# A perceiver layer on one core: time mixing taken into the attention loop, and a context copy moved from VectorE to ScalarE

## The chip, the cores and the metric

One NeuronCore of a Trainium2 chip. The time is that of one execution on the device in microseconds (us); the value for a kernel is the median of its runs. PE is TensorE, DVE is VectorE, ACT is ScalarE, POOL is GpSimd, SP is the engine that issues most DMAs.

## What is computed

The input x has 128 sequences of 32 tokens of width 128, the context 128 times 257 rows of width 96. Three residual blocks follow one another:

```python
x = x + xattn(layernorm(x), ctx)      # 16 heads, softmax over the 257 context rows
x = x + time_mix(layernorm(x))        # along the 32 tokens of a sequence
x = x + moe(layernorm(x))             # 8 experts, one is chosen for each token

# time_mix, x_prev is x shifted by one token:
k, v, r = ((x*mix + x_prev*(1-mix)) @ W.T for each of key, value, receptance)
ek = exp(k);  f_a = ek*v / a_next;  f_b = headsum(ek) / a_next
state = nan_to_num(a_pow * exclusive_cumsum(f))        # for a and b, along the tokens
out = sigmoid(r) * (state_a + eu*ek*v) / max(state_b + eu*headsum(ek), 1e-6) @ W_out.T
```

## The kernel before, in words

All 4096 tokens stay in SBUF as 32 tiles of 128 (`X`); a tile holds the 32 queries of four sequences. The five engines each have a program of their own, written out by hand; they meet at semaphores, and each engine runs its instructions strictly in the order in which they are written.

**Attention** is a loop over the 128 sequences (`pipeline`, L576; eight steps `j` = -1 to 6 in one iteration `it`, sequence n = 8*it + j). In step n PE (`pe_step`, L423) transposes the context of sequence n+2 (L360), multiplies the scores of n+1 in four tiles (L371), where the fourth tile reuses bank 0 of the first and so waits until its exponential has been taken (L369), projects the queries of n+5 into bank 3 (L383), multiplies probabilities and context of n-1 (L394, L400), in one step of four (the ones with j = 1 and 5, "projection steps") projects the output of a tile with 48 matmuls (L408), and transposes the leftovers (L449) and the probabilities of n in two halves (L416). DVE (`dve_step`, L494) copies the transposed context out of bank 7 (`dve_cT`, L533), takes the maxima (L511) and the low halves (L507, L491, L530), adds the residual of a tile (L526) and takes the statistics for the next layer norm (L623) in the step behind. ACT (`act_step`, L456) copies the high halves of the transposed probabilities (L462), takes the four exponentials (L468), and copies the queries' (L486) and the output's high halves (L477). POOL (`pool_step`, L553) normalises the probabilities (L559) and splits the context in high and low halves (L541, L545).

**Time mixing** comes after the last attention residual: tables and transposed weights (L1028 to L1039, L901 to L914, L1170 to L1183), then a pipeline over eight chunks of 512 tokens with `pe_mix` (L1041), `act_mix` (L916), `dve_mix` (L1185) and `pool_mix` (L808) in five banks of their own. Its arrays share their place in SBUF with those of the attention. Its weights are loaded early (L700 to L706), on SP's queue behind the first contexts. The expert weights are loaded once the last attention residual is done (L712 to L723).

**Routing and experts** follow: layer norm, router, sorting through DRAM, and a loop over 40 tiles of tokens with expert weights chosen at run time.

## Time and profile before

| | us |
|---|---|
| median of three runs | 1127.61 (1126.6 to 1131.02) |
| the profiled execution's own time | 1121.37 |
| its span, first to last instruction | 1119.7 |
| busy: PE, DVE, ACT, POOL | 921.9, 856.5, 665.6, 634.8 |

The page of the profile gives busy times, the chain that ended last and the costliest groups. A stretch is a window of the span, with each engine's busy time in it and the clock that PE was granted (1.00 is 2.4 GHz; 0.50 is 1.2 GHz; values between are mixtures). A timeline lists instructions with start and duration; successive ones on an engine overlap a little, so that the distance between two starts, and not the duration, is what one more of them costs. An idle time is put down to what released the engine. POOL's spans are rough.

### The profile page before, as it was taken

How to read it: one execution, taken by the hardware profiler on the slowest of the kernel's cores; microseconds unless marked ns; L12 is line 12 of the kernel's file. 1: busy time of each engine (PE TensorE's matmuls, PEld its weight loads, DVE VectorE, ACT ScalarE, POOL GpSimd, SP SyncE). 2: the span in 40 equal slices, each digit the busy share in tenths (PEclk: the TensorE clock that was granted, in tenths of full speed). 3: DMA queues.
4: the chain of work that ended last, by engine and by line, in shares of the span. 5: the costliest groups of instructions: out<-in, count | busy, mean ns of one | idle time of the engine just before them, and what ended most of it. 6: DMA issues, size and time to landing. Idle time of an engine off the chain costs nothing.

```text
span 1119.7 us, 30693 instructions
## 1 busy us (share of the span) xinstructions
PE 921.9 (82%) x9018; PEld 759.3 (68%) x9019; DVE 856.5 (76%) x2288; ACT 665.6 (59%) x1892; POOL 634.8 (57%) x983
## 2 busy tenths in 40 slices
PE   3899999999999999999999999965444436148885
PEld 3788888888888888888888888742222236136664
DVE  5888878878888887888888788757999976225543
ACT  2677767777776776777777677643121202136664
POOL 4466666665666666566566666626575510735453
PEclk9899999999999999999999999987676655659888
DMA  6100010010000001001000100039000000111110
GB/s 176 25 16 17 16 28 14 14 29 14 14 20 23 14 15 29 14 14 28 15 14 15 29 14 15 3 72 195 0 1 0 0 0 3 53 46 48 42 44 17
DMA packets 46488, 32.13 MB, mean 29 GB/s; under 512 B 6518, under 2 KB 44065, under 8 KB 46448
## 3 DMA queue, kind: packets, MB, share of 16 engines
q1 hardware_dynamic: 44144, 27.38, 10.0%
q0 software_dynamic: 2304, 4.25, 1.1%
q8 instruction: 20, 0.33, 0.1%
q14 instruction: 20, 0.16, 0.0%
HBM read 24.62 MB, written 7.52 MB: 29 GB/s over the span
## 4 chain that ended last, share of the span: by engine, by line
PE 72%; DVE 13%; issue 9%; ACT 3%; DMA 1%; POOL 1%; SPq 1%; ACTq 0%; DVEq 0%; POOLq 0%
PE bank L371 15%; PE bank L394 15%; PE bank L416 10%; PE bank L408 8%; PE bank L383 7%; DVE cs L1234 4%; PE bank L1114 4%; PE bank L1129 3%; PE bank L400 3%; PE bank L360 2%; DVE xn L656 1%; PE bank L663 1%; PE bank L1084 1%; DVE den L1225 1%; DMA wo_r<-in_L_xattn_Wo_dram 1%
## 5 line engine op out<-in xcount | busy, mean ns | idle before, releaser
L559 POOL TENSOR_TENSOR Pn<-Pe,rsum 128x1028 f32<-128x1028 f32 x128 | 243.1, 1899 | 226.6 <-DVE rsum L518 142.3
L468 ACT ACTIVATE Pe<-bank,nmax 128x257 f32<-128x257 f32 x512 | 239.5, 471 | 92.5 <-DVE nmax L511 92.4
L511 DVE TENSOR_REDUCE nmax<-bank 128x1 f32<-128x257 f32 x512 | 199.2, 409 | 1.2 <-PE bank L371 1.2
L371 PE MATMUL bank<-cT,qh 96*128 96x257 f16 x1024 | 185.2, 275 | 5.1 <-ACT Pe L468 4.1
L462 ACT ACTIVATE Th<-bank 128x512 f16<-128x512 f32 x256 | 138.9, 595 | 78.9 <-PE bank L416 78.9
L507 DVE TENSOR_TENSOR Tl<-bank,Th 128x512 f16<-128x512 f32 x256 | 172.8, 676 | 0.0
L371 PE MATMUL bank<-cT,ql 96*128 96x257 f16 x512 | 139.1, 272 | 0.0
L416 PE MATMUL bank<-identf,Pn 128*128 128x128 f32 x1024 | 133.5, 273 | 0.0
L416 PEld LDWEIGHTS bank<-identf,Pn 128*128 128x128 f32 x1024 | 109.8, 141 | 0.0
L491 DVE TENSOR_TENSOR ql<-bank,qh 96x512 f16<-96x512 f32 x128 | 87.9, 687 | 23.5 <-ACT qh L486 23.5
L468 ACT ACTIVATION_READ_ACCUMULATOR Pe<-bank,nmax 128x1 f32 x512 | 99.9, 195 | 0.0
L530 DVE TENSOR_TENSOR Ol<-bank,Oh 96x512 f16<-96x512 f32 x128 | 87.6, 685 | 12.4 <-ACT Oh L477 4.5
L371 PEld LDWEIGHTS bank<-cT,qh 96*128 96x128 f16 x1024 | 83.7, 97 | 18.8 <-issue 5.4
L383 PE MATMUL bank<-x1h,Ahi 128*96 (+1 forms) x512 | 93.5, 221 | 0.0
L383 PE MATMUL bank<-x1h,Alo 128*96 (+1 forms) x512 | 93.3, 220 | 0.0
L383 PE MATMUL bank<-x1l,Ahi 128*96 (+1 forms) x512 | 93.2, 220 | 0.0
L408 PE MATMUL bank<-Bhi,Oh 96*128 96x128 f16 x512 | 87.5, 219 | 1.5 <-DVE Ol L530 1.5
L408 PE MATMUL bank<-Bhi,Ol 96*128 96x128 f16 x512 | 87.4, 219 | 0.0
L408 PE MATMUL bank<-Blo,Oh 96*128 96x128 f16 x512 | 87.3, 219 | 0.0
L522 DVE COPY L<-bank 128x128 f16<-128x128 f16 x128 | 25.5, 200 | 73.1 <-PE bank L449 73.1
L477 ACT ACTIVATE Oh<-bank 96x512 f16<-96x512 f32 x128 | 75.8, 592 | 4.2 <-PE bank L400 3.2
L394 PE MATMUL bank<-Th,chi 128*96 128x512 f16 x256 | 76.6, 379 | 0.9 <-DVE Ol L530 0.9
(221 smaller groups left out, 2478.1 us busy)
## 6 DMA issues: line engine op xcount, KB each, us to landing
raw<-in_ctx_dram SPq DMA_DIRECT2D x32, 384.0 KB, 3.3
sorted_rows<-fill SPq DMA_DIRECT2D x1, 2620.0 KB, 20.8
xs<-sorted_rows SPq DMA_DIRECT2D x40, 65.5 KB, 1.8
R<-in_x_dram SPq DMA_DIRECT2D x4, 512.0 KB, 5.9
Z<-last_rows SPq DMA_DIRECT2D x128, 2.2 KB
w1r<-in_L_ffn_W_dram SPq DMA_DIRECT2D x8, 256.0 KB, 6.0
w2fr<-in_L_ffn_W_dram SPq DMA_DIRECT2D x8, 256.0 KB, 6.3
out_dram<-yout,idx POOLq DMA_INDIRECT x40, 2.3
```

The source lines that it names most:

```text
L371: last = nc.tensor.matmul(bank[SB[t]][:, 0:M], w[:, par, b, t * P:(t + 1) * P], cT[:, s4, c, 0:M], start=(k == 0), stop=(k == 2))
L383: last = nc.tensor.matmul(bank[b][0:CC, hh * P:(hh + 1) * P], w[:, h, :], a[:, tok], start=(k == 0), stop=(k == 2))
L394: nc.tensor.matmul(bank[6][0:CC, :], w[:, s8, c, :], p[:, par, c, :], start=(k == 0), stop=False)
L408: last = nc.tensor.matmul(bank[7][:, 512 - C:512], o[:, gp, h, :], w[:, h, :], start=(h == 0 and k == 0), stop=(h == H - 1 and k == 2))
L416: last = nc.tensor.transpose(bank[4 + c][:, t * P:(t + 1) * P], Pn[:, par, t, c * P:(c + 1) * P], identf[:, :])
L462: nc.scalar.activation(Th[:, n_par(j - 1), c, :], bank[4 + c][:, :], ACT.Copy).then_inc(s_Th, 1)
L468: nc.scalar.activation(Pe[:, n_par(j + 1), t, :], bank[SB[t]][:, 0:M], ACT.Exp, bias=nmax[:, n_par(j + 1), t:t + 1], accum_out=sums[:, n_p ...
L491: nc.vector.tensor_tensor(q_view(ql, par, c), bank[b][0:CC, :].rearrange("p (h b t) -> p h b t", h=QT, b=GB), q_view(qh, par, c), ALU.subt ...
L507: nc.vector.tensor_tensor(Tl[:, n_par(j - 1), t, :], bank[4 + t][:, :], Th[:, n_par(j - 1), t, :], ALU.subtract).then_inc(s_Tl, 1)
L511: nc.vector.tensor_reduce(nmax[:, n_par(j + 1), t:t + 1], bank[SB[t]][:, 0:M], AX.X, ALU.max, negate=True).then_inc(s_nmax, 1)
L530: nc.vector.tensor_tensor(Ol[sl], bank[6][0:CC, :].rearrange("p (h t) -> p h t", h=H), Oh[sl], ALU.subtract).then_inc(s_Ol, 1)
L559: nc.gpsimd.tensor_tensor(Pn[:, par, :, :], Pe[:, par, :, :], rsum[:, par, :].unsqueeze(2).broadcast_to([P, QT, M]), ALU.mult)\
```

## The change

Time mixing is cut into 16 chunks of 256 tokens (two tiles, eight sequences), and each chunk's operations are placed at the ends of the steps of the attention loop, one iteration for one chunk and spread over three iterations. Chunk c has its normalisation at j=3 of iteration c+1, transposes at 4, k at 5, its sum at 6, v and r at j=-1 and 0 of iteration c+2, the scans at 1 and 2, and so on to the output at j=1 of iteration c+3. PE's part lies between the two halves of the probabilities' transposes, in bank 3, which the queries' projection uses as well; that one now waits until the chunk's result has been read. The other engines' parts stand at the end of their steps. The normalisation moves from DVE to POOL, with a power and one Newton step in place of ACT's square root; DVE adds an aggregation (`bn_aggr`). The context copy moves from DVE to ACT, behind the copies of the probabilities. Tables and transposed weights are made before the loop. After the loop a remainder (`drain_mix`) runs what is left of the last chunks. The same buffers serve every chunk (the key, value and sum arrays were doubled before), and the code of the first three iterations is written out instead of one. The functions called anew are all in the diff; `...` marks lines left out.

```diff
             if exists(n + 5):
-
+                pe_mix_free(it, j)
                 pe_q(n + 5, (j + 1) % GB, bass.ds(P * (g + 1 + (jj + 1) // GB), P))
...
                 wait(nc.tensor, s_pn, n + 1)
-                pe_probsT(n, n_par(j))
+                pe_probsT(n, n_par(j), 0)
+            pe_mix(it, j, n)
+            if exists(n):
+                pe_probsT(n, n_par(j), 1)
+
+        def chunk(it, back):
+            c = it - back
+            return c if exists(c, MCH) else None
+
+        def pe_mix_free(it, j):
+
+            if j == 5 and chunk(it, 1) is not None:
+                wait(nc.tensor, s_m["xc"], it)
...
+        def pe_mix_bank(it, j, n):
+
+            if exists(n + 5):
+                wait(nc.tensor, s_ql, n + 6)
+            else:
+                wait(nc.tensor, s_ql, B)
+                pe_mix_free(it, j)
+
+        def pe_mix(it, j, n):
+            if j == 4 and chunk(it, 1) is not None:
+                c = it - 1
+                pe_mix_bank(it, j, n)
+                wait(nc.tensor, s_m["xn"], c + 1)
+                for t in range(MG):
+                    last = nc.tensor.transpose(bank[3][:, t * P:(t + 1) * P], xn2[:, t, :], identf[:, :])
+                last.then_inc(s_m["xT"], 1)
+            if j == 5 and chunk(it, 1) is not None:
+                c = it - 1
+                pe_mix_bank(it, j, n)
+                wait(nc.tensor, s_m["xc"], c + 1)
+                nc.tensor.matmul(bank[3][:, 0:MT], wka[:, :], xT33[:, :, 1:N + 1], start=True, stop=False)
+                nc.tensor.matmul(bank[3][:, 0:MT], wkb[:, :], xT33[:, :, 0:N], start=False, stop=True)\
+                    .then_inc(s_m["k"], 1)
...
+                nc.tensor.matmul(bank[3][:, 0:MT], blk[:, :], ek[:, :], start=True, stop=True).then_inc(s_m["sum"], 1)
...
+                nc.tensor.matmul(bank[3][:, 0:MT], w2T[:, 1, :], xm[:, 0, :], start=True, stop=True).then_inc(s_m["v"], 1)
...
+                nc.tensor.matmul(bank[3][:, 0:MT], w2T[:, 2, :], xm[:, 1, :], start=True, stop=True).then_inc(s_m["r"], 1)
...
+                for t in range(MG):
+                    last = nc.tensor.matmul(bank[3][:, t * P:(t + 1) * P], oT[:, t * P:(t + 1) * P], w2T[:, 3, :],
+                                            start=True, stop=True)
+                last.then_inc(s_m["y"], 1)
...
                     nc.scalar.activation(Th[:, n_par(j - 1), c, :], bank[4 + c][:, :], ACT.Copy).then_inc(s_Th, 1)
+            if exists(n + 2):
+                act_cT(n + 2, (j + 2) % 4)
...
+            act_mix(it, j)
+
+        def act_cT(n, s4):
+            wait(nc.scalar, s_ctxT, n + 1)
+            nc.scalar.activation(cT[:, s4, :, 0:MC * P], bankh[7][0:CC, 0:2 * MC * P].rearrange("p (s m) -> p s m", s=2),
+                                 ACT.Copy).then_inc(s_cT, 1)
...
+        def act_mix(it, j):
...
+                wait(nc.scalar, s_m["xT"], c + 1)
+                nc.scalar.activation(xT33[:, :, 1:N + 1], time(bank[3][:, 0:MT]), ACT.Copy).then_inc(s_m["xc"], 1)
...
+                wait(nc.scalar, s_m["ekv"], c)
+                wait(nc.scalar, s_m["k"], c + 1)
+                nc.scalar.activation(ek[:, :], bank[3][:, 0:MT], ACT.Exp).then_inc(s_m["ek"], 1)
+                wait(nc.scalar, s_m["xm"], 2 * c)
+                wait(nc.scalar, s_m["dx"], c + 1)
+                for k in range(2):
+                    last = nc.scalar.activation(mdx[:, k, :], dx[:, :], ACT.Copy, scale=mix[:, 1 + k:2 + k])
...
+                wait(nc.scalar, s_m["sum"], c + 1)
+                nc.scalar.activation(esum[:, :], bank[3][:, 0:MT], ACT.Copy).then_inc(s_m["esum"], 1)
...
+                wait(nc.scalar, s_m["r"], c + 1)
+                nc.scalar.activation(er[:, :], bank[3][:, 0:MT], ACT.Exp, scale=-1.0).then_inc(s_m["er"], 1)
+                wait(nc.scalar, s_m["dm"], c)
+                wait(nc.scalar, s_m["er"], c + 1)
+                nc.scalar.activation(er1[:, :], er[:, :], ACT.Copy, bias=1.0).then_inc(s_m["er1"], 1)
...
             moments = jj == 2 and exists(g - 1, G)
             if moments:
                 wait(nc.vector, s_res, g)
-            if exists(n + 2):
-                dve_cT(n + 2, (j + 2) % 4)
-            if moments:
-                dve_stats(g - 1)
-
+                wait(nc.vector, s_m["mv"], g - 2)
+                wait(nc.vector, s_m["xd"], it - (1 if j == 2 else 0))
...
+                if kind == "max" and t == 0 and moments:
+                    nc.vector.bn_stats(stats2[:, 1 - gp, :],
+                                       X[:, bass.ds(g - 1, 1), :].rearrange("p o c -> p (o c)")).then_inc(s_m["stat"], 1)
...
+            if moments:
+                wait(nc.vector, s_m["stat"], g)
...
+            if moments:
+                nc.vector.bn_aggr(mv[:, 1 - gp, :], stats2[:, 1 - gp, :]).then_inc(s_m["mv"], 1)
+            dve_mix(it, j)
+
+        def dve_mix(it, j):
+            if j == 2 and chunk(it, 3) is not None:
...
+                for t in range(MG):
+                    nc.vector.bn_stats(stats[:, bass.ds(MG * c + t, 1), :].rearrange("p o s -> p (o s)"),
+                                       X[:, bass.ds(MG * c + t, 1), :].rearrange("p o c -> p (o c)")).then_inc(s_m["stat3"], 1)
+            if j == -1 and chunk(it, 2) is not None:
...
+                wait(nc.vector, s_m["v"], c + 1)
+                nc.vector.tensor_tensor(ekv[:, :], ek[:, :], bank[3][:, 0:MT], ALU.mult).then_inc(s_m["ekv"], 1)
+            if j in (1, 2) and chunk(it, 2) is not None:
+                c, k = it - 2, j - 1
+                wait(nc.vector, s_m["st"], 2 * c)
+                wait(nc.vector, s_m["fab"], 2 * c + k + 1)
+                for b in range(MS):
+                    last = nc.vector.tensor_tensor_scan(cs[:, k, b, 1:N + 1], onesn[:, :], fab[:, k, b * N:(b + 1) * N],
+                                                        0.0, ALU.mult, ALU.add)
...
+                wait(nc.vector, s_m["y"], c + 1)
+                xc = X[:, bass.ds(MG * c, MG), :]
+                nc.vector.tensor_tensor(xc, xc, bank[3][:, 0:MT].rearrange("p (t c) -> p t c", t=MG), ALU.add)\
+                    .then_inc(s_m["res"], 1)
+            if j == 3 and chunk(it, 2) is not None:
...
+                    nc.vector.tensor_scalar(scl[:, k, :], sraw[:, k, :], -FMAX, FMAX, ALU.max, ALU.min)\
+                        .then_inc(s_m["scl"], 1)
...
+                    nc.vector.scalar_tensor_tensor(sst[:, k, :], sraw[:, k, :], FMAX, scl[:, k, :],
+                                                   ALU.is_le, ALU.mult).then_inc(s_m["sst"], 1)
+            if j == 4 and chunk(it, 2) is not None:
...
+                nc.vector.scalar_tensor_tensor(den[:, :], esum[:, :], nlw[:, 1:2], sst[:, 1, :], ALU.mult, ALU.add)\
...
+                nc.vector.scalar_tensor_tensor(num[:, :], ekv[:, :], nlw[:, 1:2], sst[:, 0, :], ALU.mult, ALU.add)\
...
+                nc.vector.scalar_tensor_tensor(denm[:, :], den[:, :], 1e-6, er1[:, :], ALU.max, ALU.mult)\
+                    .then_inc(s_m["dm"], 1)
+            if j == 5 and chunk(it, 2) is not None:
...
+                wait(nc.vector, s_m["dm"], c + 1)
+                nc.vector.reciprocal(rec[:, :], denm[:, :]).then_inc(s_m["rec"], 1)
...
+        def pool_mix(it, j):
+            if j == 3 and chunk(it, 1) is not None:
+                c = it - 1
+                wait(nc.gpsimd, s_m["mv"], MG * (c + 1))
...
+                nc.gpsimd.tensor_tensor(vep[:, :], mv[:, :, 1], consts[:, 0, :], ALU.add).then_inc(s_m["rs"], 1)
+                nc.gpsimd.tensor_tensor(xd[:, :, :], X[:, bass.ds(MG * c, MG), :],
+                                        mv[:, :, 0:1].broadcast_to([P, MG, C]), ALU.subtract).then_inc(s_m["xd"], 1)
+                wait(nc.gpsimd, s_m["rs"], r + 1)
+                nc.gpsimd.tensor_tensor(rs0[:, :], vep[:, :], consts[:, 1, :], ALU.pow).then_inc(s_m["rs"], 1)
+                nc.gpsimd.tensor_tensor(rsv[:, :], vep[:, :], consts[:, 1, :], ALU.mult).then_inc(s_m["rs"], 1)
+                wait(nc.gpsimd, s_m["rs"], r + 3)
+                nc.gpsimd.tensor_tensor(rsq[:, :], rs0[:, :], rs0[:, :], ALU.mult).then_inc(s_m["rs"], 1)
+                wait(nc.gpsimd, s_m["rs"], r + 4)
+                nc.gpsimd.tensor_tensor(rsv[:, :], rsq[:, :], rsv[:, :], ALU.mult).then_inc(s_m["rs"], 1)
+                wait(nc.gpsimd, s_m["rs"], r + 5)
+                nc.gpsimd.tensor_tensor(rsc[:, :], rsv[:, :], consts[:, 2, :], ALU.add).then_inc(s_m["rs"], 1)
+                wait(nc.gpsimd, s_m["rs"], r + 6)
+                nc.gpsimd.tensor_tensor(rst2[:, :], rs0[:, :], rsc[:, :], ALU.mult).then_inc(s_m["rs2"], 1)
+                wait(nc.gpsimd, s_m["rs2"], c + 1)
+                wait(nc.gpsimd, s_m["xd"], c + 1)
+                nc.gpsimd.tensor_tensor(xn2[:, :, :], xd[:, :, :], rst2[:, :].unsqueeze(2).broadcast_to([P, MG, C]),
+                                        ALU.mult).then_inc(s_m["xn"], 1)
+            if j == 5 and chunk(it, 1) is not None:
...
+                nc.gpsimd.tensor_tensor(time(dx[:, :]), xT33[:, :, 1:N + 1], xT33[:, :, 0:N], ALU.subtract)\
+                    .then_inc(s_m["dx"], 1)
+            if j == 6 and chunk(it, 1) is not None:
...
+                for k in range(2):
+                    nc.gpsimd.tensor_tensor(time(xm[:, k, :]), time(mdx[:, k, :]), xT33[:, :, 0:N], ALU.add)\
...
+                wait(nc.gpsimd, s_m["ekv"], c + 1)
+                nc.gpsimd.tensor_tensor(time(fab[:, 0, :]), time(ekv[:, :]), over_seqs(iap[:, 1:N + 1]), ALU.mult)\
+                    .then_inc(s_m["fab"], 1)
+                wait(nc.gpsimd, s_m["esum"], c + 1)
+                nc.gpsimd.tensor_tensor(time(fab[:, 1, :]), time(esum[:, :]), over_seqs(iap[:, 1:N + 1]), ALU.mult)\
+                    .then_inc(s_m["fab"], 1)
+            if j in (1, 2) and chunk(it, 2) is not None:
...
+                nc.gpsimd.tensor_tensor(time(sraw[:, k, :]), cs[:, k, :, 0:N], over_seqs(apw[:, 0:N]), ALU.mult)\
+                    .then_inc(s_m["st"], 1)
+            if j == 6 and chunk(it, 2) is not None:
...
+                nc.gpsimd.tensor_tensor(oT[:, :], num[:, :], rec[:, :], ALU.mult).then_inc(s_m["o"], 1)
...
-            for j in range(-1, 7):
-                step(0, j)
-            with eng.Fori(1, B // 8 - 1) as it:
+            for i in range(3):
+                for j in range(-1, 7):
+                    step(i, j)
+            with eng.Fori(3, LIT - 1) as it:
                 for j in range(-1, 7):
                     step(it, j)
-            for j in range(-1, 10):
-                step(B // 8 - 1, j)
+            for j in range(-1, 7):
+                step(LIT - 1, j)
+            for j in range(-1, 2):
+                step(LIT, j)
+
+        def drain_mix(step):
+            for j in range(2, 7):
+                step(LIT, j)
+            for j in range(-1, 7):
+                step(LIT + 1, j)
+            for j in range(-1, 3):
+                step(LIT + 2, j)
...
+            drain_mix(pool_step)
...
+            act.wait_ge(s_w2T, 1)
+            nc.scalar.activation(w2T[:, :, :].rearrange("p a c -> p (a c)"), bank[3][:, :], ACT.Copy).then_inc(s_w2Tc, 1)
+            act.wait_ge(s_w2, 16 * (7 + 2 * HS))
+            nc.scalar.activation(nlw[:, :], dcy[:, :], ACT.Exp).then_inc(s_texp, 1)
+            act.wait_ge(s_tdve, 2)
+            act.wait_ge(s_tab, 1)
+
+            nc.scalar.activation(apw[:, :], tt[:, :], ACT.Exp, scale=nlw2[:, 0:1])\
+                .then_inc(s_texp, 1)
+            act.wait_ge(s_m["zero"], 2)
             pipeline(nc.scalar, act_step)
...
+            drain_mix(act_step)
+
+
+            act_std(2)
...
-            pipeline(nc.tensor, pe_step)
...
             pe.wait_ge(s_w2, 16 * (7 + 2 * HS))
             for a in range(4):
-                last = nc.tensor.transpose(bank[1][:, a * P:(a + 1) * P], w2r[:, a, :], identf[:, :])
+                last = nc.tensor.transpose(bank[3][:, a * P:(a + 1) * P], w2r[:, a, :], identf[:, :])
             last.then_inc(s_w2T, 1)
+            pe.wait_ge(s_w2Tc, 1)
+            pe.wait_ge(s_tab, 5)
+            pe.wait_ge(s_m["w"], 2)
+            pipeline(nc.tensor, pe_step)
+            pe.wait_ge(s_res, G)
...
+            drain_mix(pe_step)
...
+            dve_tables()
             pipeline(nc.vector, dve_step)
-
-
-            dve.wait_ge(s_res, G)
-            dve_stats(G - 1)
-            dve_var(chain, LS)
+            drain_mix(dve_step)
+
+
+            dve.wait_ge(s_m["stat3"], G)
+            dve_var(chain, LS - G)
             dve_rstd(chain, 2)
```

## Rows read from the trace of the kernel before

**Rows 1.** Stretches: us, then each engine's busy us (instructions), clock, DMA share, GB/s.

```profile
100.00:400.00 300.00, 299.50 (x3253) 258.04 (x3252) 254.82 (x641) 227.16 (x671) 190.21 (x333) 1.00 0.06 18
...
800.00:900.00 100.00, 44.33 (x108) 24.32 (x108) 99.83 (x286) 19.17 (x32) 58.66 (x41) 0.66 0.00 0
...
1040.00:1050.00 10.00, 8.48 (x87) 6.88 (x86) 5.07 (x18) 6.34 (x21) 4.28 (x6) 0.83 0.16 48
```

**Rows 2.** Timeline where the attention ends: start, us, instruction, idle before and releaser.

```profile
744.03 0.29 DVE L526 TENSOR_TENSOR R<-R,bank 128x128 f32<-128x128 f32 x1 [3.02 <-PE bank L408]
```

**Rows 3.** The chain that ended last, in the time-mixing stage: start, us, what.

```profile
773.36 1.72 PE bank L1051 x2
...
911.10 0.88 DVE stats L623 x4
```

**Rows 4.** Timeline of PE, one step of the attention loop.

```profile
413.03 0.28 PE L360 MATMUL bank<-ident,chi 128*96 128x128 f16 x2
...
414.93 0.40 PE L371 MATMUL bank<-cT,qh 96*128 96x257 f16 x2
...
416.84 1.04 PE L416 MATMUL bank<-identf,Pn 128*128 128x128 f32 x8
417.73 0.28 PE L360 MATMUL bank<-ident,chi 128*96 128x128 f16 x2
```

**Rows 5.** Timeline of DVE, a projection step's end and the same plain step.

```profile
402.74 0.23 DVE L522 COPY L<-bank 128x128 f16<-128x128 f16 x1 [2.31 <-PE bank L449]
...
413.53 0.41 DVE L535 COPY cT<-bank 96x512 f16<-96x512 f16 x1
413.86 0.74 DVE L511 TENSOR_REDUCE nmax<-bank 128x1 f32<-128x257 f32 x2
...
417.62 0.69 DVE L530 TENSOR_TENSOR Ol<-bank,Oh 96x512 f16<-96x512 f32 x1
```

**Rows 6.** Timeline of ACT, the same step.

```profile
414.31 0.48 ACT L468 ACTIVATE Pe<-bank,nmax 128x257 f32<-128x257 f32 x1 [0.42 <-DVE nmax L511]
414.68 0.19 ACT L468 ACTIVATION_READ_ACCUMULATOR Pe<-bank,nmax 128x1 f32 x1
...
415.56 0.47 ACT L468 ACTIVATE Pe<-bank,nmax 128x257 f32<-128x257 f32 x1 [0.24 <-DVE nmax L511]
...
416.99 0.59 ACT L477 ACTIVATE Oh<-bank 96x512 f16<-96x512 f32 x1
417.49 1.09 ACT L462 ACTIVATE Th<-bank 128x512 f16<-128x512 f32 x2
```

**Rows 7.** Timeline of POOL, the work that the same step ends with.

```profile
417.49 1.90 POOL L559 TENSOR_TENSOR Pn<-Pe,rsum 128x1028 f32<-128x1028 f32 x1 [1.04 <-DVE rsum L518]
419.47 0.21 POOL L566 TENSOR_TENSOR e12p<-Pn,one 128x8 f16<-128x8 f32 x1
419.76 0.20 POOL L569 TENSOR_TENSOR e12p<-Pn,e12p 128x4 f16<-128x4 f32 x1
...
420.99 0.19 POOL L551 COPY cT<-c256T 96x2 f16 x1
```

**Rows 8.** Groups of instructions by form, 770 to 925 us: busy us, mean ns.

```profile
L1234 DVE TENSOR_TENSOR_SCAN cs<-onesn,fab 128x32 f32<-128x32 f32 x227 | 40.0, 255 | 0.0
L1228 DVE RECIPROCAL rec<-den 128x512 f32<-128x512 f32 x8 | 26.8, 3353 | 0.3
...
L835 POOL TENSOR_TENSOR xm<-mdx,xT 128x512 f32<-128x512 f32 x12 | 16.5, 1393 | 0.0
...
L1209 DVE SCALAR_TENSOR_TENSOR sst<-sraw,scl 128x512 f32<-128x512 f32 x16 | 10.3, 680 | 0.0
...
L937 ACT ACTIVATE mdx<-dx,mix 128x512 f32<-128x512 f32 x12 | 7.9, 711 | 0.0
```

**Rows 9.** One line's instructions (the denominator's product): ns min/median/max, first and last start.

```profile
L1225 DVE SCALAR_TENSOR_TENSOR den<-den,er x8: 683/1584/1584, 778.0 to 902.7; 128x512 f32<-128x512 f32 x8
```

**Rows 10.** Timeline of the SP queue, the last loads before the loop.

```profile
35.68 5.01 SPq L706 DMA_DIRECT2D dcy<-n_L_attn_time_first_dram  x8
```

370 lines of the change are left out of this document (154 added, 216 removed).

## The prediction, made before the change was run

> **What bounds the kernel now.** I read the page first, then stretches, the hand-over between the stages, and last one step of the attention loop on each engine. Inside the loop PE is busy for 299.50 of 300 us at full clock (2.4 GHz); from 800 to 900 us it is DVE that never rests (99.83 of 100 us), while PE works less than half of the time at a granted clock of 0.66, parts at 2.4 and parts at 1.2 GHz [rows 1]. So there are two stages with two bounds. The time-mixing stage lies between the residual of the last attention tile at 744.03 [rows 2] and the end of the last statistics at 911.10 + 0.88 [rows 3]: **168.0 us**, with nothing of the attention beside it. That is all the change can take away.
>
> One step of the loop, counted from its first context transpose (413.03 = 0; the next step begins at 417.73): period **4.70**, the last score tile at 1.90, the transposes of the probabilities from 3.81 to 4.70 [rows 4]. A step with the output projection has 48 matmuls more, start to start 0.056, so 2.7 us. Eight steps are 43.3 us. Three things matter for any work added here.
> - The last score tile reuses the bank of the first and waits for its exponential, which starts at 1.28 and whose accumulator read ends at 1.84 [rows 6]; PE comes free of the queries' projection at 1.89. **There is no slack:** whatever makes the first exponential late by x stops PE for x.
> - DVE: the context copy begins at 0.50, the first maximum at 0.83, the last subtraction at 4.59; marginal cost of the copy 0.33 [rows 5]. Without it DVE could start the maximum at 0.53 (0.49 and the hand-over). The exponential follows its start by 0.45, so it must start by about 0.82: DVE has 0.3 us to give per step. In a projection step DVE idles 2.31 us before its copy of the leftovers, but work placed at the end of a step comes behind that wait.
> - ACT: idle 0.42 before the first exponential and 0.24 before the third [rows 6]. Its 96x512 copy costs 0.50 (416.99 to 417.49).
>
> POOL's work of a step runs from 417.49 to 421.18, that is 3.69 of 4.70 us, and lies across the step boundary (from -0.24 to 3.46) [rows 7].
>
> **The context copy on ACT.** 0.50 fits into 0.66 idle; behind the two probability copies it ends at about 1.26, where the first exponential started anyway. Nothing gained or lost in a plain step, and ACT has no slack left. It removes a small delay in the step behind a projection, where DVE had statistics in front of the first maximum: -0.3 per eight steps.
>
> **PE's share of a chunk.** A 512-column f32 matmul is two instructions that took 1.72 us at half clock [rows 3], so 256 columns take 0.43 at full. Five of them (2.13), two transposes (the eight of a step take 4.70 - 3.81 = 0.89: 0.22), and two 128-column output matmuls (0.43): **2.8 us** per eight steps.
>
> **Stalls in a full iteration**, prices halved from [rows 8], each as the lateness of the next first exponential.
> - j=-1, ekv on DVE: 0.35, less than DVE's slack and PE's longer step: 0.
> - j=0: ACT waits for r, then er and, dependent, er1. Probability copies start at 0.52 instead of -0.24: **0.75** (0.4 to 0.8).
> - j=1: eight scans at 0.18 and a residual of 0.35 on DVE; maximum at 1.75, 0.93 too late. Beside POOL the scans take 0.24: 1.4. I take **1.2**.
> - j=2: aggregation, two statistics and eight scans, 2.1: 1.8, beside POOL 2.25. I take **2.0**.
> - j=3: two clamps and two selections, 1.05 to 1.55: **1.0** (0.5 to 1.3).
> - j=4: POOL's normalisation is nine operations, seven of them tiny and mostly dependent; POOL starts a dependent tiny one 0.29 after another (419.47 to 419.76) [rows 7]. With two 256-column operations of 0.6 to 0.7 (half of 1393 ns [rows 8]): 3.2 us from 3.46, ready at 6.7, while PE wants it at about 5.3. The power has no row; between 0.2 (a tiny one) and 0.8. Wait **1.2** (0.3 to 2). den, num and denm (1.2 to 2.4) hide mostly in it; **0.3** is left, also for ACT's copy.
> - j=5: on ACT ek behind k, then two mdx of some 0.37 (half of 711 ns [rows 8]) that wait for POOL's dx, which ends some 0.65 into the next step: **1.6** (0.9 to 1.9). The reciprocal on DVE, half of 3353 ns [rows 8], is 0.45 late and hidden by this; without that cover it costs 0.45.
> - j=6: esum on ACT behind the sum: **0.3**.
>
> These are 8.35; low ends 4.7, high ends 10.5. With PE's 2.8 and the -0.3 a full iteration grows by **10.85 us**, and 13 of the 16 are full: 141. Partial ones, by the same terms: the first with a chunk (only j=3 to 6) 4.9, the next (no output matmuls, residual or statistics) 9.7, the three last steps 3.0. Together **158.6**.
>
> POOL beside DVE: denm takes 683 ns alone and mostly 1584 ns beside POOL [rows 9]; that is the upper end above. The Trainium skill ("GPSIMD Engine Reference", Key points) says that the engine shares its SBUF interfaces with VectorE and collides with VectorE instructions with two SBUF inputs; by that rule scans, selections and the three denominators would all be slow beside the normalisation of the probabilities, and the sum would stand near its high ends. The trace agrees for denm.
>
> **Before and behind the loop.** Weights and tables must now be ready first. The last decay load is issued at 40.69 [rows 10], lands some 2 us later, when the loop begins (43.3), so loads cost little; but transposes (0.7), copy (0.6), table load (1.28), exponentials, reciprocal and two scalings (some 2) then stand in a row in front of PE: **4.5** (3 to 6; the table load was hidden before). Behind the loop the last chunk runs alone: POOL's tables and normalisation 7, transposes and copy 1.3, k at half clock 1.7, ek and sum 1.6, xm and v 1.9, ekv and fab 1.8, two rounds of scans and scalings 4.4, clamps to denominators 2.4, reciprocal 1.8, oT 0.7, output and residual 1.4, statistics 0.5: **26.5** (22 to 34). The expert weights' loads begin after the attention as before and have 60 us instead of 200; they needed about 35 us, so nothing.
>
> **Sum:** 158.6 + 4.5 + 26.5 - 168.0 = **+21.6 us**. The profiled execution took 1121.4 (span 1119.7), so 1143; it lies 6.2 below the median of 1127.6, to which I add: **1149**. Low ends: 105 + 3 + 22 - 168 = -38, 1090. High ends: 195 + 6 + 34 - 168 = +67, 1195.
>
> **Rivals.**
> 1. *The engines soak the chunk up; faster.* The place is the wait of the last score tile. If stalls are at their low ends (256-column operations cheaper than halved rows, POOL's chain in time), the iteration grows by 7.2: **1090**. It decides where an iteration grows by less than (168.0 - 26.5 - 4.5 - 17.6) / 13 = 9.2 us; my sum is 1.65 above that. For it: DVE's whole demand would be about 43 of 54 us, ACT's less; so a little run-ahead pays. Against: DVE and ACT work in order, and the added work stands just in front of the tightest hand-over. If only PE's 2.8 counted it would be 1035, which I hold for unlikely.
> 2. *The clock.* PE would be busy 46 of 54 us, 85%. In a stretch of the expert stage at 85% (8.48 of 10 us) it had 0.83 of full clock [rows 1], so parts at 1.2 GHz. PE's 46 us at that clock, less what the stalls cover, are 3.5 more per iteration: **1195**. Against: dense bursts of 4 us between the gaps. [...]
> 3. *ACT becomes the bound everywhere,* as the moved copy doesn't fit: 0.1 to 0.2 in 128 steps, **1168**. For: 0.02 us of slack. Against: the sum of the row starts just fits.
>
> **Chances.** Forecast 0.37, rival 1 0.38 (its middle at 1090, spread over both sides of it), rival 2 0.15, rival 3 0.10. About 0.5% (5.6 us) is what a measurement of this kernel can tell from no change. Faster by more than that: 0.34 of rival 1 and 0.02 of the forecast, 0.36. Within: 0.04 and 0.05, 0.09. Slower: 0.30 + 0.15 + 0.10, 0.55. The signs are both likely; the forecast's own range is 1125 to 1175. The range for 8 in 10 is 1078 to 1195: the low side holds rival 1 with half of its error, the high side the forecast's high ends and rival 2.
>
> **What would show it.** Right: the loop's steps at j=2, 3, 5 of an iteration longer by 1 to 2 us, with PE waiting for ACT's first exponential; that one waiting for DVE's maximum after j=1 to 3, and for ACT's own queue after j=0 and 5; PE waiting for POOL's normalised chunk at j=4; an iteration of 54 us; PE 85% busy in the loop; some 27 us between the last attention residual and the last statistics; the loop beginning 4.5 us later. Wrong: an iteration under 52 us (rival 1), a granted clock under 0.95 in the loop (rival 2), or plain steps longer than 4.75 (rival 3).

## The result, and the profile after

The changed kernel takes **1167.97 us** (median of four runs, 1163.18 to 1169.5); the kernel before, on the same chip, 1127.11 (1121.29 to 1131.02). The ratio is 1.036 with a 95% interval of 1.0304 to 1.0415: slower, by 40.9 us. The forecast was 1149, the range 1078 to 1195.

The profiled execution took 1169.27 us, its span is 1167.5 (before: 1121.37 and 1119.7). Where the spans' 47.8 us are:

| stretch | before | after | difference | forecast |
|---|---|---|---|---|
| start to first step of the loop | 43.6 | 52.8 | +9.2 | +4.5 |
| loop, to the last attention residual | 700.4 | 875.9 | +175.5 | +158.6 |
| time mixing behind the loop | 168.0 | 30.3 | -137.7 | -141.5 |
| rest | 207.7 | 208.5 | +0.8 | 0 |

About 5 of the first row's 9.2 us are not the change's: the same setup matmuls took longer in this execution, at the lower level of the clock (last section). The second row holds 3 us of the clock too. PE stood still ahead of the first step, and that step then began at the lower level:

```profile
52.84 0.42 PE L377 MATMUL bank<-ident,chi 128*96 128x128 f16 x2 [3.90 <-issue]
```

```profile
52.30:62.50 10.20, 8.88 (x58) 7.33 (x59) 4.08 (x11) 6.17 (x18) 3.45 (x6) 0.50 0.01 2
```

Iteration 0 has no chunk in it and still took 42.66 us, where it took 39.65 before.

Stretches of the loop, columns as in [rows 1]; the first row answers to the first there:

```profile
100.00:400.00 300.00, 262.27 (x2708) 219.44 (x2706) 238.08 (x612) 215.22 (x616) 199.05 (x356) 1.00 0.06 16
400.00:700.00 300.00, 260.32 (x2637) 215.66 (x2636) 240.63 (x608) 210.01 (x600) 195.92 (x353) 0.99 0.05 15
```

PE, busy 299.50 of 300 us before, now has some 38 us of gaps in 300; no other engine is full, DVE is even less busy than before (254.82). The granted clock is 1.00 and 0.99 in these stretches, nearly all of the time the upper level. What opens the gaps, from the waits of 400 to 700 us (engine, line, what it waited for: us, times, longest):

```profile
PE bank L388 <- ACT Pe L555: 34.2, 33, 1.8
ACT Pe L555 <- DVE nmax L633: 30.1, 48, 2.1
PE bank L505 <- POOL xn L791: 5.2, 6, 1.1
ACT er L600 <- PE bank L528: 2.8, 5, 0.6
```

PE waits for ACT's first exponential, and ACT for DVE's first maximum. One step (j=3 into j=4) on four engines. PE, where in [rows 4] the last score tile came 1.90 after the step's start, then DVE, ACT and POOL, which answer to [rows 5 to 7]:

```profile
839.35 0.28 PE L377 MATMUL bank<-ident,chi 128*96 128x128 f16 x2
...
843.03 0.40 PE L388 MATMUL bank<-cT,qh 96*128 96x257 f16 x2 [1.63 <-ACT Pe L555]
...
846.62 0.41 PE L505 MATMUL bank<-identf,xn 128*128 128x128 f32 x2 [1.06 <-POOL xn L791]
```

```profile
839.24 0.69 DVE L657 TENSOR_TENSOR Ol<-bank,Oh 96x512 f16<-96x512 f32 x1
839.84 1.52 DVE L696 TENSOR_SCALAR scl<-sraw 128x256 f32<-128x256 f32 x2
841.29 0.76 DVE L701 SCALAR_TENSOR_TENSOR sst<-sraw,scl 128x256 f32<-128x256 f32 x2
841.97 0.74 DVE L633 TENSOR_REDUCE nmax<-bank 128x1 f32<-128x257 f32 x2
...
846.33 0.47 DVE L708 SCALAR_TENSOR_TENSOR den<-esum,nlw,sst 128x256 f32<-128x256 f32 x1
846.72 2.12 DVE L711 SCALAR_TENSOR_TENSOR num<-ekv,nlw,sst 128x256 f32<-128x256 f32 x1
848.77 0.42 DVE L716 SCALAR_TENSOR_TENSOR denm<-den,er 128x256 f32<-128x256 f32 x1
```

```profile
842.41 0.48 ACT L555 ACTIVATE Pe<-bank,nmax 128x257 f32<-128x257 f32 x1 [1.74 <-DVE nmax L633]
```

```profile
839.12 1.90 POOL L750 TENSOR_TENSOR Pn<-Pe,rsum 128x1028 f32<-128x1028 f32 x1 [2.24 <-DVE rsum L643]
...
843.83 0.70 POOL L779 TENSOR_TENSOR rs<-vep,consts 128x2 f32<-128x2 f32 x1
...
845.86 0.61 POOL L791 TENSOR_TENSOR xn<-xd,rst 128x256 f32<-128x256 f32 x1
846.43 2.13 POOL L750 TENSOR_TENSOR Pn<-Pe,rsum 128x1028 f32<-128x1028 f32 x1
```

Here the last score tile comes 3.68 after the step's start, 1.78 late. DVE had scl and sst between its last subtraction and the first maximum. The first two scl take 1.52 us and end at 841.36, 0.34 behind the end of POOL's Pn (839.12 + 1.90 = 841.02). num takes 2.12 us and ends 0.28 behind the next Pn (848.84 and 848.56). The same num over the whole run: shortest, median and longest in ns:

```profile
L711 DVE SCALAR_TENSOR_TENSOR num<-ekv,nlw,sst x16: 471/2120/2121, 182.7 to 953.2; 128x256 f32<-128x256 f32 x16
```

Ten of the 16 are held, 1.65 us beyond num's own 0.47. Of the other six, one belongs to the first chunk and two to the drain; in the other three den, just ahead of num, was the one held (1.17 and twice 1.7 us for 0.47). The subtraction Ol, which reads PSUM, runs beside Pn in its usual 0.69.

### The profile page after: what moved, and what is told of

It is laid out like the page before. It is cut to its first block, busy times and chain, and to the rows that moved or that the text cites. A ratio compares the mean times of both kernels' runs of the same rounds, so it can differ in the third digit from the quotient of the medians.

```text
span 1167.5 us, 31247 instructions
## 1 busy us (share of the span) xinstructions
PE 935.8 (80%) x9098; PEld 772.6 (66%) x9099; DVE 832.9 (71%) x2229; ACT 731.2 (63%) x2072; POOL 687.1 (59%) x1194
## 4 chain that ended last, share of the span: by engine, by line
PE 33%; POOL 25%; issue 20%; ACT 9%; DVE 8%; POOLq 1%; DMA 1%; ACTq 1%; SPq 1%; DVEq 0%
POOL Pn L750 11%; PE bank L411 7%; PE bank L388 4%; PE bank L425 4%; PE bank L1269 3%; POOL chi L732 3%; ACT Pe L555 2%; PE bank L432 2%; PE bank L1284 2%; POOL sorted_rows L1073 2%; ACT Th L547 2%; POOL e12p L757 1%; DVE nmax L633 1%; PE bank L917 1%; PE bank L400 1%
## 5 line engine op out<-in xcount | busy, mean ns | idle before, releaser
L750 POOL TENSOR_TENSOR Pn<-Pe,rsum 128x1028 f32<-128x1028 f32 x128 | 246.5, 1926 | 258.5 <-DVE rsum L643 220.3
L633 DVE TENSOR_REDUCE nmax<-bank 128x1 f32<-128x257 f32 x512 | 203.3, 412 | 42.5 <-PE bank L388 41.1
L432 PE MATMUL bank<-identf,Pn 128*128 128x128 f32 x1024 | 147.8, 273 | 0.0
L432 PEld LDWEIGHTS bank<-identf,Pn 128*128 128x128 f32 x1024 | 115.0, 142 | 5.9
L555 ACT ACTIVATION_READ_ACCUMULATOR Pe<-bank,nmax 128x1 f32 x512 | 102.8, 201 | 0.0
```

What stands on the lines that cost most here:

```text
L432: last = nc.tensor.transpose(bank[4 + c][:, t * P:(t + 1) * P], Pn[:, par, t, c * P:(c + 1) * P], identf[:, :])
L555: nc.scalar.activation(Pe[:, n_par(j + 1), t, :], bank[SB[t]][:, 0:M], ACT.Exp, bias=nmax[:, n_par(j + 1), t:t + 1], accum_out=sums[:, n_p ...
L633: nc.vector.tensor_reduce(nmax[:, n_par(j + 1), t:t + 1], bank[SB[t]][:, 0:M], AX.X, ALU.max, negate=True).then_inc(s_nmax, 1)
L750: nc.gpsimd.tensor_tensor(Pn[:, par, :, :], Pe[:, par, :, :], rsum[:, par, :].unsqueeze(2).broadcast_to([P, QT, M]), ALU.mult)\
```

## The experiments

The experiments ran in three groups, each on a chip of its own beside the kernel before. That kernel's medians there were 1128.04 (copy_alone, copy_back, scans_early, clamps_mid), 1130.04 (scans_mid, norm_split, act_late, spread) and 1127.8 us (dve_only, spread2, spread3, spread3_back). The changed kernel itself was measured only once, with the result above. The ratios have 95% intervals of about half a per cent to either side, so that 5 us between two experiments is the least that the medians alone can show, and across groups some us more. Where two medians are close I give beside them the *long stretch*, from the loop's first step to the end of the last statistics, read from the profiled executions: 906.2 us in the changed kernel and 868.3 in the one before. It leaves out the setup, which differs from one execution to the next (last section). Step lengths are medians over eleven iterations of the distances between PE's first context transposes:

```text
                 5     6    -1     0     1     2     3     4    iteration (mean of 13)
changed       9.23  6.65  5.65  5.34  8.54  5.19  6.80  7.95    55.20
copy_back     9.89  6.18  5.36  5.35  8.07  5.54  7.14  7.96    55.48
scans_early   9.22  6.64  5.65  5.34  9.87  4.81  4.90  7.95    54.11
scans_mid     9.22  6.65  5.65  5.34  8.54  4.78  4.90  7.96    52.80
clamps_mid    9.09  7.17  5.65  5.34  8.54  5.19  6.80  7.87    55.94
norm_split    9.64  6.65  5.65  5.34  8.54  5.19  6.80  6.86    54.57
act_late      9.22  5.78  5.36  5.34  7.98  5.19  6.80  7.95    53.56
dve_only      9.49 10.89  5.65  5.34  8.55  4.78  5.26  8.55    57.64
spread        8.41  5.46  5.37  5.34  7.98  4.78  5.26  6.77    49.56
spread2       8.27  5.47  5.36  5.34  7.99  4.78  5.26  5.94    48.37
spread3       8.27  5.47  5.36  5.35  7.98  4.78  5.25  5.94    48.35
spread3_back  8.27  5.55  5.37  5.34  7.82  4.87  5.58  5.93    48.69
```

My theory was that the stalls are a matter of order: work in front of DVE's first maximum or ACT's first exponential, lengthened by POOL's Pn. The rivals: the copy on ACT is what costs, or the amount of work is, in whatever order.

### The copy alone (copy_alone, copy_back)

```diff
 # copy_alone: the kernel before, act_step, behind the two copies Th
+            if exists(n + 2):
+                wait(nc.scalar, s_ctxT, n + 3)
+                nc.scalar.activation(cT[:, (j + 2) % 4, :, 0:MC * P], ..., ACT.Copy).then_inc(s_cT, 1)
 # and dve_step
-                dve_cT(n + 2, (j + 2) % 4)
```

> The kernel before, with the copy of the transposed context moved from DVE to ACT behind its copies of the probabilities, and nothing else. Theory (the copy fits into gaps that ACT has in a plain step, and the end-of-step work of the time mixing is what costs): the step stays at 4.70 us, the time within 6 us of 1127. Rival (ACT bounds the step once it has the copy): each of some 130 steps grows by 0.1 to 0.3 us, 1140 to 1165.

Measured: **1121.07**, ratio 0.9958 (0.9935 to 0.998). copy_back is the reverse edit on the changed kernel (`act_cT` out, `dve_cT` in at the start of DVE's step).

> The changed kernel with the copy of the context back on DVE, at the start of DVE's step. Theory (DVE's work between its last and its next maximum is what makes the last score tile late): about 0.6 us more of DVE in front of the first maximum of each step that follows mixing work, 0.3 to 0.6 us in 7 of 8 steps, 13 iterations: 27 to 55 us slower than the changed kernel, 1195 to 1222. Rival (the copy on ACT is what the change costs): faster than the changed kernel, 1125 to 1150.

Measured: **1173.51**, 5.5 us slower than the changed kernel. The long stretch is 862.9 us in copy_alone and 911.9 in copy_back, 5.5 shorter and 5.7 longer than without the edit. The move of the copy is worth 5 to 7 us, in both kernels, for the good: the rival falls. But so does my price for DVE's copy, 27 to 55 us. A step of copy_alone on ACT:

```profile
415.68 0.59 ACT L465 ACTIVATE cT<-bank 96x512 f16<-96x512 f16 x1
416.17 0.48 ACT L473 ACTIVATE Pe<-bank,nmax 128x257 f32<-128x257 f32 x1
```

The copy ends where the exponential would have begun, as worked out. The step behind a projection step went from 4.89 to 4.69 us, the others from about 4.70 to 4.68; four steps went from 21.66 to 21.42, and 32 such fours are 8 us. On DVE the copy costs 0.33 us from start to start [rows 5], not the 0.6 that I wrote; and where ACT's own queue was last, taking the copy off ACT shortened the step (0.47, 0.29 and 0.47 us in j=6, -1 and 1), which pays for most of what was lost in j=5, 2 and 3 (0.66, 0.35 and 0.34).

### The scans (scans_early, scans_mid)

Both put a chunk's sixteen scans into step j=1, where DVE idles 2.67 us before L12.

```diff
             if exists(n + 1):
+                # scans_mid: all 16 scans here, if j == 1
                 wait(nc.vector, s_exp, QT * (n + 2))
                 wait(nc.vector, s_pn, n)
                 nc.vector.reciprocal(rsum[...], sums[...]).then_inc(s_rs, 1)
             if exists(n):
+                # scans_early: all 16 scans here, if j == 1
                 wait(nc.vector, s_left, n + 1)
```

> The changed kernel with all sixteen scans in front of DVE's wait for L12 in step j=1, where it is idle for 2.67 us. Theory: the step after j=2 loses its 2.11 us of lateness and the one after j=1 up to 0.7 us: 2.1 to 2.8 us an iteration, 27 to 39 us in all, 1129 to 1141. Rival (the order of DVE's work does not matter, PE's added work or its clock does): under 6 us of change. In the trace the scans should take about 1.03 us for eight, since Pn of POOL has ended by then.

> The changed kernel with the sixteen scans of a chunk in step j=1 again, but between the difference of the queries and the reciprocal of the sums, so that POOL's Pn starts behind them instead of beside them. scans_early had them right behind that reciprocal: its step j=1 grew from 8.54 to 9.87 us, j=2 and j=3 fell by 0.38 and 2.65. Theory (DVE's reads of SBUF stand still while Pn runs): the scans now take 1.03 us for eight, j=1 stays under 8.8 us and j=2, j=3 keep their gain, 2.5 to 3.0 us an iteration against the changed kernel, 1128 to 1136. Rival (Pn is now late itself and the columns and transposes that wait for it follow): no better than scans_early, 1144 or more.

Measured: **1144.14** and **1131.72** (ratios 1.017 and 1.0014). The order of two things on DVE is worth 12 us by these medians, which come from two chips; the ratios are 1.6% apart, 13 iterations of 1.31 us are 17 us, and the long stretches (886.6 and 867.7) are 19 us apart. Timeline of DVE, first scans_early and then scans_mid:

```profile
804.04 0.16 DVE L643 RECIPROCAL rsum<-sums 128x4 f32<-128x4 f32 x1
804.13 4.83 DVE L671 TENSOR_TENSOR_SCAN cs<-onesn,fab 128x32 f32<-128x32 f32 x16
```

```profile
842.96 1.95 DVE L671 TENSOR_TENSOR_SCAN cs<-onesn,fab 128x32 f32<-128x32 f32 x16
844.84 0.14 DVE L644 RECIPROCAL rsum<-sums 128x4 f32<-128x4 f32 x1
```

The reciprocal is what POOL's Pn waits for. Behind it, the scans start together with Pn and take 4.83 us; ahead of it, 1.95. In scans_early POOL's row says when: Pn 804.37 for 1.91 us, then the columns and the context preparation until 808.25; one scan lasted 1908 ns there, the length of Pn. This is the cleanest measurement of the case: the same sixteen instructions, 2.88 us apart, by what POOL does beside them. My number for scans_early (27 to 39 us) missed at 24, because I let the scans run "since Pn has ended by then": Pn had just begun.

### The clamps and denominators (clamps_mid)

scl and sst in j=4 and den, num, denm in j=5, ahead of the difference of the queries (`dve_q`).

> The changed kernel with the same DVE work for the clamps (scl, sst in j=3 by way of a place before the difference of the queries in j=4) and for den, num, denm (same place in j=5). Theory (DVE's instructions on SBUF are held while POOL's Pn runs): there Pn has ended, so scl x2 takes 0.6 us for 1.52 and num 0.47 for 2.12; the lateness of 1.78 and 0.98 us falls by 1 to 2 us an iteration together, 13 to 26 us in all, 1142 to 1155. Rival (only the amount of DVE work counts, wherever it stands): under 6 us of change, and the durations of scl and num stay.

Measured: **1175.18**, 7 us slower than the changed kernel, where my theory had 13 to 26 faster. The durations did what the theory says: two scl 0.49 us for 1.52, and num:

```profile
L685 DVE SCALAR_TENSOR_TENSOR num<-ekv,nlw,sst 128x256 f32<-128x256 f32 x6 | 2.9, 479 | 0.0
```

But no time came of it. The waits of 400 to 700 us name the wait that took over:

```profile
PEld bank L388 <- ACT Pe L555: 28.7, 27, 2.3
PE bank L388 <- ACT Pe L555: 24.3, 21, 2.2
PE bank L505 <- POOL xn L794: 16.7, 6, 2.8
```

PE's wait for the normalised chunk in j=4 grew from 1.1 to 2.8 us. POOL's chain to xn had stood in the shadow of DVE's lateness; take that away and PE waits at the next thing, and j=4 stays at 7.9 us. Nor is the place itself free: what stands ahead of ql and rsum makes them late, and Pn behind them, and POOL's dx behind that. ACT's wait for dx in 400 to 700 us went from 2.1 to 4.5 us, and j=6 grew by 0.52 us; 13 times that is about the 7 us.

### POOL's normalisation and ACT's order, each alone (norm_split, act_late)

norm_split moves vep, the power and rsv from the end of POOL's step j=3 to that of j=2. act_late moves four reads of bank 3 behind the next step's Th, and the two mdx and er1 into idle time:

```diff
+            act_late(it, j)        # xT at j=5, ek at j=6, esum at j=-1, er at j=1
             if exists(n + 2):
                 act_cT(n + 2, (j + 2) % 4)
...
             act_mix(it, j)         # now only mdx at j=5 and er1 at j=1
 # pool_mix
-            if j == 5 and chunk(it, 1) is not None:      # dx
+            if j == 4 and chunk(it, 1) is not None:
```

> The changed kernel with POOL's normalisation spread: its variance, power and product in j=2, the rest in j=3. PE's transposes of xn waited 1.06 us for POOL in j=4. Theory A (that wait is a stall of its own, beside DVE's): it goes, 1.0 to 1.2 us an iteration, 13 to 16 us in all, 1152 to 1155. Theory B, from clamps_mid, where DVE had nothing behind j=3 and PE then waited 2.8 us for xn with the same iteration: xn's lateness and DVE's run in parallel (num is held until 848.8 all the same), so that removing one alone brings under 6 us, 1162 to 1168.

> The changed kernel with ACT's mixing work moved: its reads of bank 3 (xT, ek, esum, er) stand behind its copies of the probabilities of the next step instead of ahead of them, the two scaled differences (mdx) ahead of ek in ACT's idle 3.46 us of j=5, er1 in its idle 2.53 us of j=1; POOL's dx goes to j=4. Theory: the step after j=5 begins its first exponential 1.2 us earlier (ek and mdx no longer ahead of Th), then limited by DVE's 1.66 us reciprocal; the one after j=0 0.4 us earlier: 1.2 to 1.6 us an iteration, 16 to 21 us, 1147 to 1152. Rival (ACT is never last, DVE's maxima are): under 6 us.

Measured: **1161.76** and **1147.46**. norm_split is 6 us faster by the medians of two chips, 0.8% or 9 us by the ratios, 8 by 13 iterations and 10 by the long stretch (895.8). That lies between the 13 to 16 of theory A and the under 6 of theory B, and neither number is right. PE's wait for xn is gone and j=4 falls by 1.09 us. But j=5 takes back 0.41, since Pn now starts ahead of den and holds it instead of num. POOL first, then DVE:

```profile
839.71 1.90 POOL L750 TENSOR_TENSOR Pn<-Pe,rsum 128x1028 f32<-128x1028 f32 x1 [0.34 <-DVE rsum L643]
```

```profile
840.45 1.45 DVE L708 SCALAR_TENSOR_TENSOR den<-esum,nlw,sst 128x256 f32<-128x256 f32 x1
841.82 0.47 DVE L711 SCALAR_TENSOR_TENSOR num<-ekv,nlw,sst 128x256 f32<-128x256 f32 x1
```

num is at its own 0.47 in all 16 here. act_late, 20.5 us, is as expected: 0.87, 0.29 and 0.56 us in j=6, -1 and 1.

### Everything of DVE alone (dve_only)

scans_mid, and scl in j=3, sst in j=4, den, denm and rec in j=5, num in j=6, all ahead of rsum.

> The changed kernel with only DVE's part of spread (scans in j=1, scl in j=3, sst in j=4, den, denm, rec in j=5, num in j=6, all ahead of the reciprocal of the sums), POOL's scaled sums in j=1; ACT and POOL's normalisation as in the changed kernel. Theory (stalls of engines that run side by side don't add): scans_mid brought 36 us, the other DVE work stood in steps where ACT's ek and mdx (j=5) and POOL's xn (j=4) are late as well, so it brings only 5 to 20 us more, 1112 to 1127, and PE's wait for xn grows from 1.06 us to over 2.5. Rival (DVE's order is all of it): within 10 us of spread, 1083 to 1093.

Measured: **1203.19**, slower than everything else, where my theory had 1112 to 1127; of that theory only the longer wait for xn came, 3.2 us. Step j=6 takes 10.89 us for 6.65. Timelines of DVE, POOL, ACT and PE:

```profile
593.48 1.75 DVE L702 RECIPROCAL rec<-denm 128x256 f32<-128x256 f32 x1
595.14 0.12 DVE L644 RECIPROCAL rsum<-sums 128x4 f32<-128x4 f32 x1
```

```profile
595.35 1.90 POOL L756 TENSOR_TENSOR Pn<-Pe,rsum 128x1028 f32<-128x1028 f32 x1 [4.35 <-DVE rsum L644]
...
598.98 0.61 POOL L803 TENSOR_TENSOR dx<-xT 128x256 f32<-128x256 f32 x1
```

```profile
596.51 0.38 ACT L584 ACTIVATE ek<-bank 128x256 f32<-128x256 f32 x1 [3.45 <-PE bank L512]
599.69 0.91 ACT L588 ACTIVATE mdx<-dx,mix 128x256 f32<-128x256 f32 x2 [2.80 <-POOL dx L803]
600.50 1.06 ACT L547 ACTIVATE Th<-bank 128x512 f16<-128x512 f32 x2
```

```profile
602.55 0.40 PE L388 MATMUL bank<-cT,qh 96*128 96x257 f16 x2 [3.81 <-ACT Pe L555]
```

Read it in that order: den, denm and rec make rsum 2.8 us later; Pn follows rsum; POOL's dx follows Pn and the preparation; ACT's mdx waits 2.80 us for dx; Th, the copy of the context and the first exponential are queued behind mdx; PE stands still for 3.81 us. PE's granted clock falls in this loop, here behind that gap:

```profile
595.00:600.00 5.00, 3.74 (x39) 3.33 (x37) 2.20 (x8) 0.69 (x2) 4.01 (x7) 1.00 0.00 0
600.00:605.00 5.00, 2.45 (x9) 1.38 (x10) 3.13 (x7) 4.34 (x14) 0.00 (x0) 0.83 0.00 0
```

PE had no matmul from about 598.7 to 602.55; then the clock is 0.83, a mixture of the two levels. Over 400 to 700 us it is 0.94; clamps_mid, with gaps of 2.8 us, has 0.97, all others at least 0.98. A gap of 3.8 us isn't needed for a fall: in this loop some came behind gaps of 2.7 to 3.2 us, and in the changed kernel's loop two came behind gaps of 1.82 (at 448 and 670 us), while ten more such gaps in it brought none.

### All three together, and what was left (spread, spread2, spread3, spread3_back)

spread is act_late, norm_split and dve_only in one kernel. With dx already at j=4, what wrecked dve_only isn't there.

> norm_split and act_late together, scans as in scans_mid, and DVE's other mixing work in the same place between the difference of the queries and the reciprocal of the sums: scl in j=3, sst in j=4, den, denm and rec in j=5 (where DVE has 2.3 us idle), num in j=6; POOL's two scaled sums in j=1. Theory (order and cover decide, not amount): every step but the two with a projection at 4.7 to 5.1 us, an iteration of 47 to 49.5 us for 55.2, 75 to 105 us less than the changed kernel, 1065 to 1095, under the kernel before. Rival 1 (the engines are full: DVE 240 and POOL 200 of 300 us busy, PE 260): not under 52 us an iteration, 1127 or more. Rival 2 (TensorE's clock falls once the loop is tight): granted clock under 0.95 in the loop.

Measured: **1082.59**, ratio 0.9582 (0.9517 to 0.9646). Alone the three gave -20.5, -6 and +35 us, together -85. The iteration of 49.56 us just misses the 47 to 49.5 expected. What remained in the waits was xn again (1.7 us an iteration). spread2 puts the second part of the normalisation ahead of POOL's preparation in j=3; spread3 adds this:

```diff
-            dve_tables()
-            pipeline(nc.vector, dve_step)
+            pipeline(nc.vector, dve_step, dve_tables)    # tables() behind iteration 0, so too for ACT and PE
...
-            ... POOL's tables for the routing ...
-            drain_mix(pool_step)
+            drain_mix(pool_step, pool_tables)            # behind the step j == 3 of the drain
```

> spread, with the second part of POOL's normalisation in j=3 ahead of its preparation of the context blocks (1.3 us) instead of behind it. In spread PE waited 1.7 to 1.9 us in j=4 for xn and hardly for anything else. Theory (that wait is now a stall of its own, as nothing of DVE or ACT runs beside it): 1.3 us an iteration less, 48.2 us for 49.6, 15 to 18 us less than spread, 1064 to 1068. Rival (another engine is as late in j=4, as when norm_split moved the same wait alone and brought 6 us): under 5 us, 1078 or more.

> spread2, with the tables for the time mixing (exponentials of the decay, their reciprocal, the scaled key weights) after iteration 0 of the loop instead of ahead of it, and POOL's tables for the routing behind the normalisation of the last chunk. Ahead of the loop those tables took 3.9 us from the copy of the weights to the first transpose, of which ACT's table load of 1.28 us stays; behind the loop they stood 1.5 us in front of the last normalisation. Theory: 2.6 us and 1.5 us, 4 us less than spread2. Rival (the tables now stand in front of steps of the loop and cost there what they cost before): no difference.

Measured: **1067.48** and **1063.83**. The ratio of spread3 is 0.9449 (0.9408 to 0.9489): 5.5% faster than the kernel before and 104 us faster than the changed one. The 3.65 us between the two are less than the medians can show, and the profile bears out only a part of them. From the end of the weights' copy to PE's next transpose it is 0.05 us instead of 3.26. But the tables then cost the same wait behind iteration 0, which is what the rival said of them:

```profile
92.18 0.40 PE L377 MATMUL bank<-ident,chi 128*96 128x128 f16 x2 [3.39 <-DVE wkb L1330]
```

What is left is the drain: from the last attention residual to the last statistics 25.7 us, in spread2 27.0, in the changed kernel 30.3. From the last context transposes ahead of the loop to the last statistics spread3 is 1.0 us shorter than spread2 (807.8 and 808.8). spread3's loop, 400 to 700 us:

```profile
400.00:700.00 300.00, 294.83 (x3024) 245.13 (x3021) 257.89 (x709) 243.21 (x692) 222.52 (x407) 1.00 0.06 16
```

PE is again busy for 98%, and DVE, ACT and POOL carry 17, 33 and 27 us more in 300 than in the changed kernel: the same work in less time.

> spread3 with the copy of the context back on DVE. In the changed kernel this cost only about 5 us. Theory A (DVE is near full in a plain step once its mixing work stands inside the steps, 4.05 us of its own and 0.5 to 0.8 of mixing in 4.7 to 5.0): 0.5 us more in four to six of eight steps, 26 to 40 us slower than spread3. Theory B (the copy costs the same 5 us wherever the mixing stands, since PE bounds the steps): 3 to 8 us slower.

Measured: **1069.36**, 5.5 us slower, theory B. DVE is then busy 271.62 of 300 us, and ACT waits 35.5 us for the maxima instead of 13.4, yet PE is busy for 292.82 us, hardly less.

## Why the forecast came out as it did

Its sign and its mechanism were right: the chunk's work cannot be soaked up where it stands, since it stands in front of the first maximum and the first exponential. It had given "slower" a chance of 0.55, so the sign was no strong call. The time was 19 us too low. The sum stood at 1143 against the profiled 1121.4 of before; the changed kernel's profiled execution took 1169.3, 26 more. Of these the loop has 17, the start 5 and the drain 4. The start's 5 lie in setup matmuls that the change doesn't touch: in the one execution PE reached the upper clock level at 20 us, with a fall from 30 to 37, in the other only at 42 (last section). No term of the forecast could have had them, and that they add to the misses of the loop is chance. The two profiled executions lay 6.2 below and 1.3 above their medians, which gives back 7.

**The loop.** An iteration grew by 11.9 us (55.20 less the 43.3 of eight steps before), not by 10.85; 13 times the difference is 14 of the 17 us. The other 3 are iteration 0 at the lower clock level, for which the forecast had no term. In spread3_back, whose iteration 0 ran at the upper level, it took 43.04 us, which is the 39.65 of before and the 3.39 of the wait for the tables. The first iteration with a chunk grew by 5.6 us for a forecast of 4.9, the next by 10.3 for 9.7. The lateness of the last score tile, behind each j, forecast against measured in one iteration:

| behind j | -1 | 0 | 1 | 2 | 3 | 4, xn | 4 | 5 | 6 | sum |
|---|---|---|---|---|---|---|---|---|---|---|
| forecast | 0 | 0.75 | 1.2 | 2.0 | 1.0 | 1.2 | 0.3 | 1.6 | 0.3 | 8.35 |
| measured | 0 | 0.72 | 0.36 | 2.11 | 1.78 | 1.06 | 0.98 | 1.52 | 0.52 | 9.05 |

The terms that were too small are j=3 and j=4, by 0.78 and 0.68 us: "two clamps and two selections, 1.05 to 1.55: 1.0" and "hide mostly in it; 0.3 is left". I had the effect in [rows 9] and took the middle of the two prices; measured, it is mostly the upper one, because the reciprocal that starts Pn stands just ahead of the end of DVE's step. num was held in 10 of 16 and den in three of the others. The clamps, with one SBUF input, were held too, which I hadn't expected. Against that, the scans of j=1 fell behind Pn's end, at 0.12 us each and not 0.18, so that this term was 0.84 too large: part of the errors cancelled, which is luck. The Trainium skill ("SBUF — State Buffer", Who interferes with whom) says that a VectorE instruction with two SBUF inputs contends with a GpSimd instruction that reads SBUF, that one in a 2-port mode, which `tensor_scalar` can enter, contends with GpSimd too, and that whichever was issued first blocks the other for its whole length. The trace agrees: 2.12 us for 0.47, an instruction held for 1908 ns beside a Pn of 1.91, and Ol, one of whose inputs is in PSUM, not held. Which mode the clamps ran in no view shows. By that rule taken at its word the forecast would have stood at its high ends in j=3 and j=4, as I wrote then and did not follow.

**The drain** took 30.3 us for a forecast of 26.5, inside its 22 to 34. **The start**: from the last context transposes ahead of the loop to the first step it was 2.0 us before (41.64 to 43.63) and is 6.3 now (46.54 to 52.84), 4.3 for a forecast of 4.5. Here the term was right; the lower clock behind it is in iteration 0 above. **The power**, which had no row, is 0.70 us, in its bounds of 0.2 to 0.8.

**The copy** was priced at -0.3 us per eight steps; it is -0.5 in the kernel before (two fours of 0.24), and some 0.3 an iteration in the others (55.20 to 55.48, 48.35 to 48.69).

**The rivals.** In the full iterations the clock stayed at 0.99 to 1.00, though PE was 87% busy: the case of 1195 is out. But the clock did fall: in iteration 0, for 3 us of time, and twice in the loop behind gaps of 1.82 us, which made those two iterations 55.86 us long instead of 55.35. How far the wait for the tables brought on the fall in iteration 0 no run isolates; copy_alone, which has no such wait, had a shorter one there (53.0 to 56.4 us) and the kernel before none. ACT as the bound in every step is out by copy_alone; the 1168 that it gave is the measured time by another way. "The engines soak the chunk up" is false for this order and true for another: it decided at 9.2 us an iteration, and spread3 is at 5.1 (48.35 less 43.3) with the same operations on the same engines. So the stalls that I priced were real, but they were the price of this order and not of the work.

What no run settles: whether DVE's own Pn-bound instructions or the late Pn makes up the last 2.3 us by which spread3's iteration exceeds the loop of before and PE's share of 2.8, and how much of the drain a shorter chain would give.

## What to carry to other kernels

When a stage is woven into a tight loop of in-order engines, ask of each added instruction what is queued behind it, and put it behind the hand-over the others wait for (the copies, the maxima) but ahead of the instruction that starts a long POOL operation; amount matters less than place, 104 us here. Stalls that run side by side do not add: removing one alone showed 6 to 20 us or a loss, removing three 85, so look at which wait takes over before you give up an edit. And never put a wait for a slow neighbour (mdx for dx) in front of the work that the loop turns on.
